# Cross-attention scores from 32-row quarters in one set of four banks, and the value bias added by TensorE

## The reference

```python
Q = _split_heads(query @ Wq + bq, B)      # query: layer norm of x, [16, 112, 256]
K = _split_heads(key @ Wk + bk, B)        # key = value = ctx_1024, [16, 375, 256]
V = _split_heads(value @ Wv + bv, B)
energy = jnp.einsum('bhqd,bhkd->bhqk', Q, K) / scale          # scale = sqrt(16)
energy = jnp.where(mask == 0, jnp.asarray(NEG_INF, energy.dtype), energy)
attention = jax.nn.softmax(energy, axis=1)                    # over the 16 HEADS
x = jnp.einsum('bhqk,bhkd->bhqd', attention, V)
x = x.transpose(0, 2, 1, 3).reshape(B, -1, D_MODEL)
return x @ Wo + bo
```

## Time and profile before

| | |
|---|---|
| median of 3 runs | 657.27 us |
| profiled execution | 656.48 us |
| its span | 654.6 us |
| PE busy (matmul) | 553.0 us, 84% |
| DVE busy | 534.7 us, 82% |
| ACT busy | 309.5 us, 47% |
| POOL busy | 364.1 us, 56% |

### The profile page before, as it was taken

How to read it: one execution, slowest core, us unless ns; L and a number is a source line. 1 busy time by engine, 2 the same in 40 slices (tenths; PEclk the granted TensorE clock), 3 DMA queues, 4 the chain that set the end, 5 groups by cost and what they waited for, 6 DMA issues and landing times. The chain is left out here.

```text
span 654.6 us, 14337 instructions
## 1 busy us (share of the span) xinstructions
PE 553.0 (84%) x5904; PEld 380.5 (58%) x5904; DVE 534.7 (82%) x781; ACT 309.5 (47%) x505; POOL 364.1 (56%) x272
## 2 busy tenths in 40 slices
PE   4799999995799999999999999999999773666543
PEld 3677777763566666666566566766666431333222
DVE  4687888887387877898988989888998969999983
ACT  3566666662254444455444453445353352545431
POOL 6402332223266566667775886588668545596552
PEclk9999999999799999999999999999999886877765
DMA  8910000000100110111011101110110000000000
GB/s 190 301 50 2 2 3 3 2 2 1 46 1 1 52 52 9 46 52 54 8 46 52 51 4 53 53 47 10 49 52 10 1 14 1 2 16 33 10 22 34
DMA packets 18611, 23.44 MB, mean 36 GB/s; under 512 B 2997, under 2 KB 16290, under 8 KB 18546
## 3 DMA queue, kind: packets, MB, share of 16 engines
q1 hardware_dynamic: 16626, 21.73, 11.3%
q10 hardware_dynamic: 1920, 0.79, 0.6%
HBM read 18.85 MB, written 1.84 MB: 32 GB/s over the span
## 5 line engine op out<-in xcount | busy, mean ns | idle before, releaser
L1126 POOL TENSOR_TENSOR work<-work,rden 125x1792 f32<-125x1792 f32 x48 | 178.7, 3723 | 99.8 <-DVE rden L785 99.2
L976 ACT ACTIVATE work<-scores 125x896 f32<-125x896 f32 x96 | 95.1, 990 | 112.9 <-PE scores L1260 112.4
L774 DVE TENSOR_REDUCE negmax<-scores 125x56 bf16<-125x896 f32 x96 | 104.3, 1086 | 51.3 <-PE scores L1250 50.9
L783 DVE TENSOR_REDUCE den<-work 125x56 f32<-125x896 f32 x96 | 103.2, 1075 | 0.0
L1250 PE MATMUL scores<-qz,kT 64*125 64x224 f32 x768 | 89.0, 350 | 0.0
L1250 PEld LDWEIGHTS scores<-qz,kT 64*125 64x125 f32 x768 | 72.1, 184 | 0.8
L1275 PE MATMUL head_out<-work,v 125*32 125x112 f32 x1536 | 57.8, 271 | 4.1 <-POOL work L1126 3.8
L1260 PE MATMUL scores<-negmax,identb 125*125 125x448 bf16 x192 | 54.0, 362 | 6.7 <-DVE negmax L774 6.6
L1275 PEld LDWEIGHTS head_out<-work,v 125*32 125x32 f32 x1536 | 37.8, 109 | 28.6 <-issue 20.6
L785 DVE RECIPROCAL rden<-den 125x56 f32<-125x56 f32 x96 | 48.3, 503 | 3.3
L324 DVE TENSOR_REDUCE a_mpad<-a_s_ps 112x8 bf16<-112x896 f32 x32 | 33.5, 1092 | 20.7 <-PE a_s_ps L498 20.7
(11 more groups left out here) (186 smaller groups left out, 1088.7 us busy)
## 6 DMA issues: line engine op xcount, KB each, us to landing
ctx_sb<-in_ctx SPq DMA_DIRECT2D x16, 375.0 KB
mask_sb<-in_mask_Bx1xSxS_if SPq DMA_DIRECT2D x32, 164.1 KB
xsx<-in_x SPq DMA_DIRECT2D x4, 448.0 KB, 9.5
out_x<-ores SPq DMA_DIRECT2D x7, 256.0 KB, 2.2
a_raw_w<-in_L_ffn_gate_w SPq DMA_DIRECT2D x1, 1024.0 KB, 6.2
a_raw_w<-in_L_ffn_up_w SPq DMA_DIRECT2D x1, 1024.0 KB, 8.7
a_raw_w<-in_L_ffn_down_w SPq DMA_DIRECT2D x1, 1024.0 KB, 12.3
xt<-xsx SPq DMA_DIRECT2D x4, 112.0 KB, 2.2
```

The source lines that it names most:

```text
L774: dve.tensor_reduce(negmax[0:KP, u, :], scores[u][0:KP, :, 0:HM * HALF].rearrange("p a (h t) -> p t a h", h=HM), AX.XY, ALU.max, negate=Tr ...
L783: link(dve.tensor_reduce(den[0:KP, kc, half], ex2[0:KP, kc, :, half, :].rearrange("p g t s -> p t g s"), AX.XY, ALU.add))
L976: act.activation(ex2[0:KP, kc, :, u * HALF:(u + 1) * HALF, :].rearrange("p (a g) t s -> p a g s t", a=2), scores[u][0:KP, :, 0:HM * HALF]. ...
L1126: pool.tensor_tensor(ex2[0:KP, kc], ex2[0:KP, kc], over, ALU.mult).then_inc(s["prob"], 1)
```

## The change

All scores of a chunk now lie in one tensor of four banks, `scores[P, 4, 512]`, and a chunk is scored whole, not in two units of tokens. `score` makes eight penalty matmuls of 224 columns and eight fp32 matmuls of 224 columns, each on 32 rows (two heads, `qz` with one head in two); four neighbouring ones use different rows and different banks. `key_max` takes one maximum over 1792 columns and `less_max` has four matmuls. There are two exponentials per chunk, each over two banks (`half_exp`), and both half sums wait for both of them. One reciprocal (`inverse`) of 112 columns follows. With one set of banks, the penalties of the next chunk wait for the exponentials of the present one: the first four for the first exponential, the others for the second.

The value bias is cut into three bf16 parts once (`value_bias` on DVE), and a matmul of ones with them starts each value group. ACT copies the values. The FFN weights' transposes all move ahead of the first batch, into the banks of the scores; ACT and DVE copy three pieces each. `head_outputs` runs through the heads in another order. `own_queries` is one multiplication of 448 columns per batch. The x steps and `residual` move: `residual` comes a turn later, and `x_shift` with it.

```diff
-                def unit_max(q, kc, u):
-                    wait(dve, s["s_ps"], 6 * b + 2 * kc + u + 1)
-                    dve.tensor_reduce(negmax[0:KP, u, :],
-                                      scores[u][0:KP, :, 0:HM * HALF].rearrange("p a (h t) -> p t a h", h=HM),
+                def key_max(q, kc):
+                    wait(dve, s["s_ps"], 3 * b + kc + 1)
+                    dve.tensor_reduce(negmax[0:KP, :],
+                                      scores[0:KP, :, 0:4 * TOK].rearrange("p j (h t) -> p t j h", h=4),
                                       AX.XY, ALU.max, negate=True).then_inc(s["max"], 1)
                 def head_sum(q, kc, u):
-                    wait(dve, s["exp"], 6 * b + 2 * kc + u + 1)
+                    wait(dve, s["exp"], 6 * b + 2 * kc + 2)
                     link(dve.tensor_reduce(den[0:KP, kc, half], ex2[0:KP, kc, :, half, :].rearrange("p g t s -> p t g s"),
                                            AX.XY, ALU.add))
-                    dve.reciprocal(rden[0:KP, kc, half], den[0:KP, kc, half]).then_inc(s["rden"], 1)
+                def inverse(q, kc):
+                    dve.reciprocal(rden[0:KP, kc, :], den[0:KP, kc, :]).then_inc(s["rden"], 1)
...
+                def half_exp(q, kc, i):
+                    wait(act, s["sm_ps"], 6 * b + 2 * kc + i + 1)
+                    wait(act, s["pv"], 3 * b + kc - 2)
+                    act.activation(ex2[0:KP, kc, 4 * i:4 * i + 4].rearrange("p (j m) t s -> p j m s t", m=NE),
+                                   scores[0:KP, 2 * i:2 * i + 2, 0:4 * TOK].rearrange("p j (m s t) -> p j m s t", m=NE, s=2),
+                                   ACT.Exp).then_inc(s["exp"], 1)
+                def values(q):
+                    wait(act, s["v_ps"], b + 1)
+                    wait(act, s["pv"], 3 * b - 3)
+                    act.copy(v[0:KP, r, :, :, 0:3:2, :].rearrange("p k n s d -> p (k n) s d"),
+                             wide[0:KP].rearrange("p a b -> p (a b)")[:, 0:NKC * D].rearrange("p (n s d) -> p n s d", s=2, d=DH)
+                             ).then_inc(s["wide_read"], 1)
...
+                def score(q, kc):
+                    for i in range(2):
+                        wait(pe, s["exp"], 6 * b + 2 * kc - 1 + i)
+                        for u in range(2):
+                            for n in range(2):
+                                bank = scores[0:KP, 2 * i + n, 0:4 * TOK].rearrange("p (a t) -> p a t", t=TOK)
+                                pe.matmul(bank[:, :, u * HALF:(u + 1) * HALF], pen[64 * n:64 * n + HALF, r, u, kc, :],
+                                          identb[64 * n:64 * n + HALF, 64 * n:64 * n + HALF].unsqueeze(1).to_broadcast([HALF, 4, HALF]),
+                                          start=(u == 0), stop=False, skip_group_check=True)
                     for m in range(NE):
-                        for n in range(2):
-                            rows = slice(64 * n, 64 * n + 64)
+                        for j in range(4):
+                            rows = slice(32 * j, 32 * j + 32)
+                            last = pe.matmul(scores[0:KP, j % 2 * 2 + j // 2, m * 2 * TOK:(m + 1) * 2 * TOK],
                                              kT[rows, r, m, kc * KP:(kc + 1) * KP],
+                                             qz[rows, r, m].rearrange("p s t -> p (s t)"),
                                              start=False, stop=False, skip_group_check=True)
                     last.then_inc(s["s_ps"], 1)
...
                 def value(q, kc):
+                    out = wide[0:KP, kc // 2, (kc % 2) * D:(kc % 2 + 1) * D]
+                    pe.matmul(out, ones[0:65, :], bv_parts[0:65, :], start=True, stop=False)
                     for c in range(NE):
+                        last = pe.matmul(out, ctxT[:, q[1], c, kc * KP:(kc + 1) * KP], cv[:, c, :],
+                                         start=False, stop=(c == NE - 1))
```

More of the change, by code:

```diff
@@ L740, in _ @@
             def _(sp):
-                for n in range(B + 1):
+                for n in range(B + 2):
                     if n + 1 >= 2 and n + 1 < B:
@@ L896, in _ @@
                 for n in range(-1, B):
-                    new, now, old = in_turn(n + 1), in_turn(n), in_turn(n - 1)
+                    new, now, old, older = (in_turn(n + i) for i in (1, 0, -1, -2))
                     first, second, third = pair_begun(n), pair_begun(n - 1), pair_begun(n - 2)
+                    if old:
+                        head_sum(old, 2, 0)
                     if now:
-                        unit_max(now, 0, 0)
+                        key_max(now, 0)
                     if old:
                         head_sum(old, 2, 1)
-                    if third is not None:
-                        x_shifted(third)
+                        inverse(old, 2)
+                    if older:
+                        residual(older)
+                    if second is not None:
+                        x_shift(second)
                     if now:
-                        unit_max(now, 0, 1)
+                        key_max(now, 1)
                         head_sum(now, 0, 0)
-                        values(now)
+                        head_sum(now, 0, 1)
+                        inverse(now, 0)
                     if first is not None:
@@ L955, in _ @@
                     if k == 2:
+                        x_shifted(NPT - 2)
+                        x_rounded(NPT - 2)
                         x_shift(NPT - 1)
@@ L1199, in _ @@
                         output_bias(new)
+                    if now:
+                        normalise(now, 1)
                     if second is not None:
@@ L1369, in gate @@
                         pe.wait_ge(s["exp"], 6 * B - 1)
-                        wait(pe, s["small_read"], acts.value())
                     wait(pe, s["silu"], n)
```

297 lines of the change are left out of this document (140 added, 157 removed).

## The result

The changed kernel takes 685.18 us (median of 4 runs, 682.84 to 689.2), where the kernel before took 656.88 (4 runs): ratio 1.043, 95% interval 1.0372 to 1.0489. The change costs 28.3 us; the prediction had 14 and its own range ended at 684. The profiled execution took 685.62 us, its span is 683.8, so 29.2 more than before.

The account below looks back on a forecast made before the run. PE was taken to bound the cross-attention block, DVE close behind. Turns 302.6, x steps 49.7 and clock 4.4 made 356.7 against 348.3 us; with start 4.7 and tail 1, 671 us, range 640 to 686 (forecast's own 662 to 684).

Parts of the forecast that it names:

- A plain turn of 19.0 us: Cross-attention turn without x-step waits: three times 3.05 us plus 9.84 us, counted 15 times.
- the 3.05 us from a score to the subtraction: Per chunk: scores 0.93, one maximum 2.02 and two hand-overs 0.1 us, with PE's own work fitting beside.
- The other half, 9.84 forecast: From subtraction to next scores, three chunks a turn, set by PE's own work: 3.31, 3.27 and 3.26 us.
- Turn 0 at 17.6 us: First turn of the block, without old heads: three chunks of 3.05 plus 2.82 us.
- x steps, 49.7 us and 4.4 of clock: Twelve turns: DVE x steps wait for POOL's normalise, 49.7 us; PE's lower clock after eleven waits, 4.4 us.
- x_shift was put at 9.5 us: Turns 5, 7, 9, 12, 14: x_shift waits out a normalise, x_block_max adds 0.45; 1.9 us each.
- two sets of banks covered it: Kernel before: DVE steps blocked by POOL cost little because two sets of banks covered them; no size given.
- Start +4.7: Before the block: added weight transposes and ACT copies start the first scores 4.7 us later, between 3.0 and 7.
- Tail +1: FFN stage: x_shifted and x_rounded of the sixth pair move one round later; +1 us, between -2 and +3.
- Cover for the blocked steps: Rival, 25%: blocked x steps in the block find cover, so the kernel takes 635 to 646 us.
- The chain hides PE's work: Rival, 15%: PE's work fits beside the three-engine chain, a turn is 17.6 us, the kernel 657 us.
- One set of banks is worse: Rival, 10%: 0.3 us added between chain links counts 48 times, and clock falls cost 9 more; 694 us.

Follow-up runs that it names:

- e1: Changed kernel with x_shift, x_shifted, x_rounded and x_variance moved ahead of the reciprocal that releases POOL's normalise; 648.8 us.
- e5: e1 with the penalty also ahead of the reciprocal and two FFN weight copies on ACT moved ahead of the first queries; 635.1 us.
- e6: Changed kernel with x_shift alone moved ahead of the old batch's last reciprocal; 683.9 us.
- c1: Kernel before with all its x steps moved to where they come second to a normalise; 712.0 us.
- c2: Kernel before with only x_rounded moved, to behind the penalty; 679.5 us.
- c3: Kernel before with only x_shifted moved, to behind the second maximum; 671.6 us.
- e3: e1 with the penalty also ahead of the reciprocal and half of each maximum left out; 616.6 us.
- e8: e5 with the old value path: DVE adds the bias and copies the values, no bias matmuls; 633.7 us.
- e7: Changed kernel, DVE order untouched, with POOL's normalise cut into two instructions of half a chunk; 672.0 us.

## Why the prediction was half right

The direction and the mechanism were right: PE idles behind maxima that are late because x steps come second to a normalise. The forecast of 671 us was 14 too low. On the profiled execution the misses are 10.2 us in the plain turns, 7.1 in turns 0 and 1, 4.4 ahead of the block, 1.6 behind it and 0.4 between; 8.6 too much for the x steps and the clock hid part of them, which was luck. What failed is the length of a plain turn, and beside it two things that the sum put at nothing: the penalty behind turn 0's reciprocal, and the clock at the program's start. By its steps:

- *A plain turn of 19.0 us* was 19.68, and counts 15 times: 10.2 us, the largest miss. The mis-sized term is the 3.05 us from a score to the subtraction. The timeline of the first chunk of turn 2:

```profile
228.51 1.04 PE L1273 MATMUL scores<-qz,kT 32*125 32x224 f32 x16
...
229.69 2.02 DVE L786 TENSOR_REDUCE negmax<-scores 125x112 bf16<-125x1792 f32 x1 [1.00 <-PE scores L1273]
...
231.77 0.97 PE L1283 MATMUL scores<-negmax,identb 125*125 125x448 bf16 x4
...
232.58 0.27 PE L1361 MATMUL wide<-bv_parts,ones 65*125 65x256 bf16 x1
...
232.69 1.03 PE L1363 MATMUL wide<-cv,ctxT 128*125 128x256 f32 x4
...
233.65 1.01 PE L1300 MATMUL head_out<-work,v 125*32 125x112 f32 x32
...
234.59 0.60 PE L1267 MATMUL scores<-identb,pen 56*125 56x224 bf16 x8
...
235.12 0.47 PE L1273 MATMUL scores<-qz,kT 32*125 32x224 f32 x4
```

  From score to subtraction it is 3.26 us: the maximum starts 1.18 behind the scores, not 0.93 + 0.05, and is followed by 0.06. The second chunk has 3.18 and the third 3.26, 9.70 in place of 9.15. That makes 0.55 us a turn. The scores cost 0.97 to the next start, not 0.86 or 0.93. The other half, 9.84 forecast, was 9.99: head outputs cost 0.94 for 32 records (0.79 forecast), the subtraction 0.81.
- *Turn 0 at 17.6 us* was 23.4. The prediction listed the x steps behind reciprocals and overlooked the penalty, a TENSOR_SCALAR that stands in the same place in every turn. In turn 0 POOL came late and the penalty second: PE waits 4.3 us, and the clock falls behind that wait. From the penalties of turn 0 to those of turn 2 the changed kernel takes 44.35 us (forecast 36.6), e1 43.0 and e5 37.9. e5, and e1 up to its wait, ran turn 0 at full clock, and what sets these two turns apart is the penalty: 5.2 us are its price. The changed kernel's lower clock at the start of turn 0 is the 1.3 above e1, and longer links are the 1.3 that e5 has above the forecast.
- *x steps, 49.7 us and 4.4 of clock* was 45.5 in all. x_varp, which the prediction let wait against one reading of the Trainium skill, did wait, 3.3 us in each turn that begins a pair. The Trainium skill's SBUF — State Buffer, section Who interferes with whom, names tensor_scalar among the operations that can take the shared ports; the trace agrees, down to two elements a partition. x_shift was put at 9.5 us and is about 5 (e6). x_rounded was to wait in turns 6, 8, 13 and 15 and did not, as x_varp ahead of it had waited out the same normalise; only in turn 10 did it wait (4.10 us).
- *Why it was cheap before*: "two sets of banks covered it" was wrong (c1, c2, c3). It did not enter the sum, as the old turns' length was measured, but it would have misled whoever wanted to keep two sets as a cure.
- *Start +4.7* was 5.1. *Tail +1* was 2.6, inside the bounds given. The 4.4 us ahead of the block were in no term. (The prediction's sum for DVE counts 1.94 us for a maximum, beside its own 2.02; no term of the time hangs on it.)
- *The rivals.* Cover for the blocked steps: little; turns 4 to 15 lie 45.0 us above plain ones, where 49.7 and 4.4 were counted. The chain hides PE's work: no, it stands above it by 1.2 us (e3). One set of banks is worse, 694: in part, as its added time between links is there, 0.2 us a chunk and not 0.3. The Trainium skill, TensorEngine Tiling (Array Packing), section PSUM Bottleneck, warns that emptying PSUM may limit after row tiling; e3 agrees in kind, with 1.2 us a turn and not more.

The best version is e5 or e8, which can't be told apart: 635.1 and 633.7 us, about 3.5% below the kernel before. The changed kernel and e5 differ in the order of instructions alone, and 50 us lie between them; by their traces some 6 of these are the clock of the start (3.5 ahead of the block, 1.3 up to the penalties, 1.3 in turn 0), which comes and goes. No run gives the kernel before the same cure: its x_sh (up to 1.64 us) and x_r (up to 1.57) also come second to a normalise, so how much of the 3.5% the new form itself is worth stays open.

## What to carry to other kernels

An instruction on DVE that was seen to wait out POOL's belongs ahead of the instruction that releases POOL, not behind it: moving four short steps won 36 us of 685. Look for two-element operations of 3 us that end with POOL's. A step's price depends on where it stands, so a price measured in one order must not be carried to another, and every instruction in the same place has to be looked at, not only those one suspects. In a loop through several engines take the distance from start to start of two dependent instructions, not durations plus a guess for hand-overs; nearly 0.2 us in each of 45 chunks were 8 us.

## What the runs showed of the hardware that was not expected

- A TENSOR_SCALAR with one input of 128x2 fp32 waits 3.3 us behind a POOL multiplication; one of 128x750 (int32 to bf16) took 4.41 in place of 0.57 to 0.66.
- The waiting instruction gets in between two POOL instructions of 1.9 us each (e7). Not always: in turn 0 of the changed kernel the penalty began beside output_bias (202.25 to 202.90), and the normalise at 202.84 still went first; in e7 both pieces of it did (the penalty took 4.68). What decides it stays open.
- A PE wait of 3 to 5 us can cost more than itself: in c2 the eight score records behind a wait of 4.24 us took 1.70 us in place of 0.92, and some 2.5 us of added blocking cost 4.9 a turn. It need not: behind a wait of 3.27 us in turn 11 the granted clock stayed at 1.00 in the changed kernel and was 0.57 for 4 us in e6.
